# Sixteen tiles of attention's input, turned by VectorE's 32x32 blocks and transfers through DRAM instead of by TensorE

## The chip, the cores and the metric

One core of a Trainium2 chip. The metric is the device time of one execution in microseconds (us); lower is better. The kernel before takes 1691.37 us (median of three runs, 1691.37 to 1691.6).

## The reference

2048 tokens (4 sequences of 512), width 512, all float32. Each layer is added to a residual `x`:

```
x = x + 0.5*ffnA(norm(x))            # gated, hidden 2048, Walsh-Hadamard folded into W2
x = x + attn(norm(x))                # attn normalises once more, with gamma and beta, and adds its own input
x = x + 0.5*ffnA(norm(x))
x = x + 0.5*ffnB(norm(x))            # ternary weights, hidden 1408
x = x + ssm(norm(x))                 # tanh(x B^T) C^T + D x
x = x + 0.5*ffnB(norm(x))
```

with, in attention,

```
residual = x                                     # here x is norm(x) of the main path
x_norm = (x - mu) / sqrt(var + EPS) * gamma + beta
q, k, v = x_norm @ qkv ; causal softmax per sequence ; out @ o_proj + residual
```

The change concerns `x_norm` alone: attention needs it with features on the partitions, that is, turned.

## The kernel before

`x` stays in SBUF as 16 tiles of 128 tokens. A matmul in float32 quality is three passes over a high and a low part (`three`, lines L601, L603, L605), so each operand is split: ScalarE (ACT) writes the high part, VectorE (DVE) the low part (the source less the high part).

**The feed-forward passes.** `PASSES` lists eight; numbers 0 to 3 are ffnA on half the tokens each. A pass of kind A has 16 slots, one for each 128 hidden units. In a slot TensorE computes seven products of six matmuls (a Strassen-like scheme) in the order p1, p5, p6, p2, then four tiles of the down product (six matmuls each, in a ring of three PSUM banks), then p7, p3, p4. In the last slot p7, p3, p4 come ahead of the down tiles, and eight more down tiles follow. The seven products share five banks, so other engines stand between them: ACT copies BY to BW (`seed_w`, L1555) between p7 and p4, so **p4 can't start until ACT has run `seed_w`**, and ACT works its list strictly in order. Within a slot its list is `seed_y`, `hid_high`, `keep_p5`, (first normalisation), `silu_c11`, ..., (second normalisation), `seed_w`, `silu_c12`, `hid_high`. The order on every engine is that of the code; there is no planner for it. A value named `..._ready` or `..._done` is a semaphore.

**Weights** come from copies in DRAM (`w13_kept`, `w2_kept`), all through the queue of SyncE (SP), which also works strictly in order. In its iteration for slot s it loads the w13 weights of slot s+1 (896 KB of high parts in two transfers, 896 KB of low parts in one), then w2 of slot s. During pass 1 the weights of ffnB are prepared and stored as well, up to slot 12.

**The two normalisations ahead of attention** go in eight pairs of tiles, h = 0 to 7 (chunk c of attention, one sequence, is pairs 2c and 2c+1). `first_norm(h)` on ACT writes the main path's norm into `xn`; DVE's `second_stats(h)` takes its mean and variance; GpSimd (POOL) makes scale and shift and adds the norm to `x` (`y_added`); `second_norm(h)` on ACT writes attention's norm, still without gamma and beta, beside it (`xn[2:4]` for h < 4, `xnb` after). Pairs 0 to 3 are normalised in slots 12 to 15 of pass 1 (`TWICE_IN`), pairs 4 to 7 inside attention.

**Turning.** TensorE turns each tile by four 128x128 transposes against `ident` into a PSUM bank (`turn`, L937; semaphore `tt_ready`). Pairs 0 to 2 are turned in slots 13, 14, 15 (`TURNED_EARLY`) between or before down tiles, pair 3 right before the first q product, pairs 4 to 7 between attention's products (`x_turn`). ACT then applies gamma and beta in PSUM (`affine`, L1453) and writes `xt_hi` (L1460); DVE writes `xt_lo` (L2269).

**The other way of turning** is there already: after passes 0, 2 and 3, and in `s_turn` for the pass after attention, DVE transposes 32x32 blocks inside a tile (`STREAM_TRANSPOSE`), SP stores the result in DRAM and loads it back in another order of the blocks. Two tiles go together, since their elements are interleaved in pairs.

Of the kernel before, what the change touches and what calls it, by code (L numbers as in the profile page):

```python
# [8 lines left out]
F32 = mybir.dt.float32  # L9
# [6 lines left out]
P = 128  # L16
# [88 lines left out]
class Plan:  # L105
# [26 lines left out]
    def add_pass(self, no):  # L132
# [12 lines left out]
        for s in range(ps.n + 1):  # L145
# [13 lines left out]
            if no == BEFORE_T - 1:  # L159
                if s in TURNED_EARLY:  # L160
                    for j, b in enumerate((BV, BX)):
                        n = 2 * TURNED_EARLY.index(s) + j
                        self.bank["t", n] = b
                        ps.turns[s].append((n, n))
            elif no < len(PASSES) - 1 and no not in SWAPPED and s in ps.turn_slots:
# [64 lines left out]
def build(nc, t):  # L230
# [7 lines left out]
    s_scratch = nc.dram_tensor("s_scratch", [2, KD, 2 * P // BLOCK, BLOCK, P // BLOCK, 2 * BLOCK], F32).ap()  # L238
    mix_raw = nc.dram_tensor("mix_raw", [2, P, KD * D], F32).ap()
    mix_kept = nc.dram_tensor("mix_kept", [2, P, 2, KD * D], F32).ap()  # L240

    with ExitStack() as ctx:
# [52 lines left out]
        xnb = at("xnb", [P, 4, D], F32, "hid", 8 * KIB)  # L295
        s_swap = at("s_swap", [P, 2, KD, P // BLOCK, BLOCK, 2], F32, "hid", 8 * KIB)
# [58 lines left out]
        def bank(b):  # L355
# [58 lines left out]
        tt_ready, affine_ready, xt_hi_ready, xt_ready = (sem("tt_ready"), sem("affine_ready"), sem("xt_hi_ready"),  # L414
                                                         sem("xt_ready"))
# [12 lines left out]
        t_use = {("x", 1, 1): 0, ("q", 0, 0): 1, ("q", 0, 1): 2}  # L428
        for c in range(CH):
            extra = {0: [("x", 2, 0), ("q", 1, 0), ("x", 2, 1), ("q", 1, 1)],  # L430
                     1: [("x", 3, 0), ("q", 2, 0), ("x", 3, 1), ("q", 2, 1)],
                     2: [("q", 3, 0), ("q", 3, 1)], 3: []}[c]
            for key in [("v", c, 0), ("v", c, 1)] + extra:
                t_use[key] = len(t_use)
        products = [key for key in t_use if key[0] in "qv"]
        filled = {key: n + 1 for n, key in enumerate(products)}
# [156 lines left out]

        def first_norm_tile(h, j):
            return xn[:, j, :] if h < 4 else xn[:, 2 * (h % 2) + j, :]
# [19 lines left out]
        def _(sp):  # L615
# [151 lines left out]

            def s_turn(c):
# [67 lines left out]
            for ps in passes[1:]:  # L836
                if ps.no == BEFORE_T:
                    sp.wait_ge(mix_split_kept, 16 * len(MIX_IN))
                    sp.wait_ge(p4_done, T_UNITS)
                    for m in range(2):  # L840
                        sp.dma_start(mix_hi[m][:, :, :].rearrange("p k d -> p (k d)").bitcast(F32),
                                     mix_kept[m][:, 0, :]).then_inc(mix_in[m], 16)
                        sp.dma_start(mix_lo[m][:, :, :].rearrange("p k d -> p (k d)").bitcast(F32),
                                     mix_kept[m][:, 1, :]).then_inc(mix_in[m], 16)
                    for c in range(2):
                        s_turn(c)
                for s in range(ps.n):
# [45 lines left out]
        def _(pe):  # L893
# [79 lines left out]
            def first_product(ps, s, exact):  # L973
                u = ps.u0 + s
                weights_wait(ps, s, exact)
                if ps.no == BEFORE_T - 1 and s - 1 in TURNED_EARLY:
                    pe.wait_ge(xt_ready, 2 * TURNED_EARLY.index(s - 1) + 2)
# [99 lines left out]
            def turn_tiles(ps, s):  # L1077
                for n, tile in ps.turns[s]:
                    if ps.no == BEFORE_T - 1:
                        pe.wait_ge(p5_kept if plan.bank["t", n] == BV else c11_read, ps.u0 + s + 1)  # L1080
                        pe.wait_ge(xnb_ready, n + 1)
                        turn(t_tile(n), plan.bank["t", n]).then_inc(tt_ready, 1)
                    else:
                        bank_free("n", n)
                        pe.wait_ge(xn_ready, plan.norm_base[ps.no] + tile + 1)
# [1688 lines left out]
```

## Time and profile before

| | |
|---|---|
| median of three runs | 1691.37 us |
| the profiled execution | 1691.88 us |
| its span, first to last instruction | 1690.1 us |
| TensorE (PE) busy | 1681.5 us, 99% |
| VectorE busy | 1169.0 us, 69% |
| ScalarE busy | 821.5 us, 49% |
| DMA | 361.33 MB, mean 214 GB/s |

The profile is of one execution; its time outside the span is 1.8 us. A matmul's own duration (about 390 ns) overlaps its neighbours'; what a matmul costs is the distance from one start to the next, about 0.227 us for 128x512. Idle time of an engine other than TensorE costs nothing unless TensorE waits for it.

### The profile page before, as it was taken

Reading aid. Unit: us, or ns where it says so; the run is one execution under the profiler, and the core shown is the slowest. Engines: PE = TensorE matmul, PEld = TensorE weight load, DVE = VectorE, ACT = ScalarE, POOL = GpSimd, SP = SyncE. Lnnn points to the kernel's source line nnn. Section 1 sums busy time; section 2 is a strip of 40 time slices with the busy share of each in tenths; the row PEclk is TensorE's granted clock in tenths of the full one; section 3 lists DMA queues with packets and bytes.
Section 4 is the critical chain, followed back from the end, with each engine's and each line's share of the span. In section 5 each row is a group of like instructions: output and inputs, shape, how many; then the busy total and the mean of one; then the engine's idle time right before and its main releaser. Section 6 shows DMA issues by size and latency. Waiting matters only on the chain.

```text
span 1690.1 us, 21592 instructions
## 1 busy us (share of the span) xinstructions
PE 1681.5 (99%) x7579; PEld 1389.0 (82%) x7579; DVE 1169.0 (69%) x1832; ACT 821.5 (49%) x1335; POOL 125.6 (7%) x185
## 2 busy tenths in 40 slices
PE   9999999999999999999999999999999999999998
PEld 7788888888888888888888888888888888888887
DVE  8888778667776555755446655447668869877866
ACT  5745444465575543433223333223556456655644
POOL 1000000000012220000000000000000143100001
PEclk9999999999999999999999999999999999999999
DMA  9778866699985004257545457444766663366666
GB/s 319 265 309 298 288 261 230 242 366 361 369 336 212 1 1 99 96 175 224 180 154 184 153 173 239 144 160 147 254 226 206 252 224 112 131 233 240 250 222 214
DMA packets 140028, 361.33 MB, mean 214 GB/s; under 512 B 44688, under 2 KB 68112, under 8 KB 134544
## 3 DMA queue, kind: packets, MB, share of 16 engines
q1 hardware_dynamic: 139920, 359.92, 59.9%
q8 instruction: 64, 1.05, 0.3%
q14 instruction: 44, 0.36, 0.1%
HBM read 270.22 MB, written 89.65 MB: 213 GB/s over the span
## 4 chain that ended last, share of the span: by engine, by line
PE 94%; DVE 3%; DMA 1%; SPq 1%; issue 1%; ACT 0%; DVEq 0%; ACTq 0%
PE psum L601 35%; PE psum L603 30%; PE psum L605 27%; PE psum L937 1%; DMA x<-in_w2a 1%; SPq L748 1%; DVE xc_lo L2144 0%; DMA w<-w_kept 0%; DMA flat<-in_w3a 0%; PE psum L1214 0%; DVE att_lo L2113 0%; DVE fw_lo L2107 0%; SPq L704 0%; DVE x L2090 0%; DVE x L2202 0%
## 5 line engine op out<-in xcount | busy, mean ns | idle before, releaser
L601 PE MATMUL psum<-xc_hi,w 128*128 128x512 f32 x1544 | 603.8, 391 | 1.1 <-DMA w<-w_kept 0.6
L603 PE MATMUL psum<-xc_lo,w 128*128 128x512 f32 x1544 | 600.9, 389 | 0.0
L605 PE MATMUL psum<-xc_hi,w 128*128 128x512 f32 x928 | 361.2, 389 | 0.0
L601 PEld LDWEIGHTS psum<-xc_hi,w 128*128 128x128 f32 x1544 | 289.8, 188 | 66.1 <-issue 2.7
L603 PEld LDWEIGHTS psum<-xc_lo,w 128*128 128x128 f32 x1544 | 289.9, 188 | 59.2
L601 PE MATMUL psum<-w,hid 128*128 128x512 f32 x864 | 337.5, 391 | 0.0
L605 PE MATMUL psum<-w,hid 128*128 128x512 f32 x864 | 336.4, 389 | 0.0
L2186 DVE TENSOR_TENSOR x<-psum,x 128x512 f32<-128x512 f32 x256 | 173.1, 688 | 147.4 <-PE psum L605 146.8
L603 PE MATMUL psum<-w,hid 128*128 128x512 f32 x544 | 211.7, 389 | 0.0
L605 PEld LDWEIGHTS psum<-xc_hi,w 128*128 128x128 f32 x928 | 174.2, 188 | 36.4
L2210 DVE TENSOR_TENSOR hid<-sg,hid 128x512 fp32r<-128x512 f32 x212 | 144.6, 692 | 82.2 <-ACT hid L1516 79.7
L1555 ACT ACTIVATE psum<-psum 128x512 f32<-128x512 f32 x108 | 62.9, 582 | 284.8 <-PE psum L605 219.2
L601 PEld LDWEIGHTS psum<-w,hid 128*128 128x128 f32 x864 | 162.2, 188 | 36.2 <-DVE x L2186 2.7
L605 PEld LDWEIGHTS psum<-w,hid 128*128 128x128 f32 x864 | 162.2, 188 | 33.9
L1516 ACT ACTIVATE hid<-sg 128x512 fp32r<-128x512 f32 x204 | 129.3, 646 | 105.0 <-DVE sg L2236 51.9
L2227 DVE TENSOR_TENSOR sg<-psum,sg 128x512 f32<-128x512 f32 x104 | 71.6, 688 | 71.6 <-ACT psum L1555 70.8
L603 PEld LDWEIGHTS psum<-w,hid 128*128 128x128 f32 x544 | 102.2, 188 | 20.5
L2223 DVE TENSOR_TENSOR psum<-psum,sg 128x512 f32<-128x512 f32 x104 | 72.2, 695 | 42.8 <-PE psum L605 35.9
L1488 ACT ACTIVATE psum<-psum 128x512 f32<-128x512 f32 x108 | 62.8, 581 | 78.7 <-PE psum L605 53.6
L1954 POOL TENSOR_SCALAR var_eps<-meanvar 128x4 f32<-128x4 f32 x24 | 7.0, 291 | 1227.6 <-DVE meanvar L2058 854.1
L1547 ACT ACTIVATE sg<-psum 128x512 f32<-128x512 f32 x64 | 38.0, 594 | 89.2 <-PE psum L605 89.2
L1363 ACT ACTIVATE xn<-x,shift,rstd 128x512 f32<-128x512 f32 x88 | 65.7, 806 | 13.4 <-POOL shift L1957 10.0
(178 smaller groups left out, 2002.6 us busy)
## 6 DMA issues: line engine op xcount, KB each, us to landing
w<-w_kept SPq DMA_DIRECT2D x93, 896.0 KB, 6.7
w<-w_kept SPq DMA_DIRECT2D x130, 512.0 KB, 7.3
w<-w_kept SPq DMA_DIRECT2D x57, 640.0 KB, 4.5
w_kept<-w SPq DMA_DIRECT2D x16, 1792.0 KB, 7.4
w<-w_kept SPq DMA_DIRECT2D x93, 256.0 KB, 4.5
w_kept<-prep SPq DMA_DIRECT2D x12, 1792.0 KB, 7.5
w_kept<-w SPq DMA_DIRECT2D x16, 512.0 KB, 7.6
turn_scratch<-swap SPq DMA_DIRECT2D x48, 128.0 KB, 2.5
```

What stands on the lines that cost most here:

```text
L601: pe.matmul(out, a_hi, b_hi, start=start, stop=False, skip_group_check=onto)
L603: last = pe.matmul(out, a_hi, b_lo, start=False, stop=stop and zero == "a", skip_group_check=onto)
L605: last = pe.matmul(out, a_lo, b_hi, start=False, stop=stop, skip_group_check=onto)
L1363: return copy(out, x[:, i, :], AF.Identity, bias=shift[:, i:i + 1], scale=rstd[:, i:i + 1])
L1488: copy(bank(BY), bank(BX), AF.Copy).then_inc(y_seeded, 1)
L1516: copy(by_tile(hid_of(u, c)[:, 0, :], no), in_pairs(own(u) if c else sg[:, 0, :], no), AF.Copy).then_inc(hid_hi_ready, 1)
L1547: copy(sg[:, 0, :], bank(BX), AF.Silu, scale=gate_scale(ps, s)).then_inc(c11_read, 1)
L1555: copy(bank(BW), bank(BY), AF.Copy).then_inc(w_seeded, 1)
L2186: tt(at_x, b, at_x, ALU.add).then_inc(added, 1)
L2210: tt(by_tile(h[:, 1, :], no), in_pairs(source, no), by_tile(h[:, 0, :], no), ALU.subtract).then_inc(hid_ready, 1)
L2223: tt(bank(BZ), bank(BY), own(u), ALU.add).then_inc(z_seeded, 1)
L2227: tt(own(u), bank(BY), own(u), ALU.add).then_inc(c22_ready, 1)
```

## The change

All 16 tiles are turned the other way. For a pair h, now: `second_norm(h)` on ACT; `xt_swap_pair(h)` on DVE (two `STREAM_TRANSPOSE` of 128x512); `xt_store(h)` on SP (one transfer of 512 KB to `x_scratch`, in runs of 1 KB); `xt_load(h)` on SP (four transfers of 128 KB into `xt_raw`, in runs of 256 bytes); `xt_high(h)` on ACT (gamma and beta in place in SBUF by four instructions of 128x256, then one copy of 128x1024 to `xt_hi`); `xt_low(h)` on DVE (one subtraction of 128x1024). The 64 transposes on TensorE, their banks and their waits go.

```diff
+            def xt_store(h):
+                sp.wait_ge(xt_swapped, 2 * h + 2)
+                if h >= 2:
+                    sp.wait_ge(xt_in[raw_half(h - 2)], raw_loads(h - 2))
+                sp.dma_start(x_scratch[h % 2]..., xt_swap[...]...).then_inc(xt_stored[h % 2], 16)
+            def xt_load(h):
+                if h:
+                    sp.wait_ge(xt_ready, 2 * (h if h <= 4 else h - 1))
+                else:
+                    sp.wait_ge(kept2[(LAST_W2 - 1) % 4], nth(LAST_W2 - 1, 4))
+                sp.wait_ge(*stored(h))
+                for b in range(P // BLOCK):
+                    sp.dma_start(xt_raw[...]..., x_scratch[...]...).then_inc(xt_in[raw_half(h)], 16)
...
@@ SyncE, attention (mix loads: the weights of q and of v)
                     for m in range(2):
+                        if m:
+                            xt_load(3)
                         sp.dma_start(mix_hi[m]...) ; sp.dma_start(mix_lo[m]...)
+                    for h in (4, 6): store h, store h+1, load h, load h+1
@@ SyncE, pass 1
                             if s == UNITS["B"] + 1:          # slot 12
+                                xt_store(0)
                                 w2_out(LAST_W2)
+                                xt_load(0)
+                        elif s in TWICE_IN:                  # slots 13, 14, 15
+                            xt_store(TWICE_IN.index(s))
+                            if s + 1 < ps.n:
+                                xt_load(TWICE_IN.index(s))
@@ ScalarE
+            def xt_high(h):
+                act.wait_ge(xt_in[raw_half(h)], raw_loads(h))
+                for k in range(KD):
+                    last = copy(raw[:, k, :], raw[:, k, :], AF.Identity, bias=beta[...], scale=gamma[...])
...
+                copy(xt_cols(xt_hi, h), raw_cols(h), AF.Copy).then_inc(xt_hi_ready, 1)
             def first_norm(h):
...
+                if h == 5:
+                    act.wait_ge(xt_swapped, 2 * 4)
+                elif h:
+                    act.wait_ge(*stored(h - 1 if h < 5 else h - 2))
@@ ScalarE, up_slot
-                if ps.no == BEFORE_T - 1 and s in TWICE_IN:
-                    first_norm(TWICE_IN.index(s))
                 silu_c11(ps, s)
+                if ps.no == BEFORE_T - 1 and s in TWICE_IN[1:]:
+                    first_norm(TWICE_IN.index(s))
...
-                    if not last:
-                        turned_early(ps, s)
+                    if s in TURNED_EARLY and not last:
+                        xt_high(TURNED_EARLY.index(s))
                     if s in TWICE_IN and not last:
                         second_norm(TWICE_IN.index(s))
@@ VectorE, up_slot
+                if early and last:
+                    second_stats(TWICE_IN.index(s))          # ahead of sum_c22, gated
...
+                    if early and last and k < 2:
+                        xt_swap_pair(TWICE_IN.index(s), (k,)) # between the down tiles' adds
...
                     hid_low(u, 1)
+                    if early and s in TWICE_IN:
+                        xt_swap_pair(TWICE_IN.index(s))
                     hid_low(u, 0)
```

Three places of the order. ScalarE in slot 13 of pass 1, before, from the silu of the first gate (`silu_c11`) to `seed_w` (`psum<-psum`, waiting for p7_done); `psum,small` is gamma and beta, `kept...` are stores of weights:

```order
L1547 ACTIVATE sg<-psum 128x512 [waits hid_ready,p2_done]
L1453 ACTIVATE psum<-psum,small 128x128 [waits tt_ready]
L1453 ACTIVATE psum<-psum,small 128x128 x3
L1460 ACTIVATE xt_hi_78<-psum 128x4x128 [waits kept2_3,kept2_0,kept13_1,affine_ready]
L1453 ACTIVATE psum<-psum,small 128x128 [waits tt_ready]
L1453 ACTIVATE psum<-psum,small 128x128 x3
L1460 ACTIVATE xt_hi_78<-psum 128x4x128 [waits affine_ready]
L1479 ACTIVATE xn<-xn,shift_121,rstd_120 128x512 [waits tt_ready,rstd2_ready]
L1479 ACTIVATE xn<-xn,shift_121,rstd_120 128x512
L1555 ACTIVATE psum<-psum 128x512 [waits c21_read,p7_done]
```

and the same stretch of the changed kernel, in its own line numbers (L1390 is `first_norm`, L1479 and L1487 `xt_high`, L1507 `second_norm`, L1583 `seed_w`):

```order
L1575 ACTIVATE sg<-psum 128x512 [waits hid_ready,p2_done]
L1390 ACTIVATE xn<-x,shift,rstd 128x512 [waits xt_stored0,rstd_ready,stats2_ready,y_added]
L1390 ACTIVATE xn<-x,shift,rstd 128x512 [waits rstd_ready]
L1479 ACTIVATE xt_raw_85<-xt_raw_85,small 128x256 [waits xt_in0]
L1479 ACTIVATE xt_raw_85<-xt_raw_85,small 128x256 x3
L1487 ACTIVATE xt_hi_78<-xt_raw_85 128x4x256 [waits kept2_3,kept13_1,affine_ready]
L1507 ACTIVATE xn<-xn,shift_125,rstd_124 128x512 [waits xt_swapped,rstd2_ready]
L1507 ACTIVATE xn<-xn,shift_125,rstd_124 128x512
L1583 ACTIVATE psum<-psum 128x512 [waits c21_read,p7_done]
```

`first_norm` has moved behind the silu and waits for the store of the pair before; between it and `seed_w` ACT now waits for a load (`xt_in0`) where it waited for a turn of TensorE.

SyncE at slots 12 to 14 of pass 1, before (`prep` and `prep_last` are stores of ffnB's weights; `w_53` is w13, `w_54` w2):

```order
L698 DMA w_kept<-prep_68 128x1024 [waits w2_ready]
L698 DMA w_kept<-prep_last 128x1024 [waits w2_ready]
L617 DMA w_53<-w_kept 128x1280 [waits p4_done,kept13_0]
L617 DMA w_53<-w_kept 128x512
L649 DMA w_53<-w_kept 128x1792 [waits w13_lo_in0]
L663 DMA w_54<-w_kept 128x1024 [waits kept2_1,down_ready]
L617 DMA w_53<-w_kept 128x1280 [waits p4_done,kept13_1]
```

and now:

```order
L714 DMA w_kept<-prep_68 128x1024 [waits w2_ready]
L788 DMA x_scratch<-xt_swap_83 128x4x256 [waits xt_swapped]
L714 DMA w_kept<-prep_last 128x1024 [waits w2_ready]
L800 DMA xt_raw_85<-x_scratch 32x16x64 [waits xt_stored0,kept2_3]
L800 DMA xt_raw_85<-x_scratch 32x16x64 x3
L633 DMA w_53<-w_kept 128x1280 [waits p4_done,kept13_0]
L633 DMA w_53<-w_kept 128x512
L665 DMA w_53<-w_kept 128x1792 [waits w13_lo_in0]
L679 DMA w_54<-w_kept 128x1024 [waits kept2_1,down_ready]
L788 DMA x_scratch<-xt_swap_83 128x4x256 [waits xt_swapped]
L800 DMA xt_raw_85<-x_scratch 32x16x64 [waits xt_stored1,xt_ready]
L800 DMA xt_raw_85<-x_scratch 32x16x64 x3
```

The loads of the weights for slot 14 (the first L633) and slot 15 stand behind a wait for a store to land.

## Rows read from the trace of the kernel before

**Rows 1.** The page: busy time by engine, and the granted clock in 40 slices.

```profile
PE 1681.5 (99%) x7579; PEld 1389.0 (82%) x7579; DVE 1169.0 (69%) x1832; ACT 821.5 (49%) x1335; POOL 125.6 (7%) x185
...
PEclk9999999999999999999999999999999999999999
```

**Rows 2.** TensorE's timeline (start us, us, what, [idle before]): the warming matmuls.

```profile
1.33 5.06 PE L1298 MATMUL psum<-warm 128*128 128x512 f32 x11 [1.33 <-POOL warm L1931]
```

**Rows 3.** TensorE's timeline in slot 13: a turn between matmuls; start of p4.

```profile
496.83 0.39 PE L605 MATMUL psum<-w,hid 128*128 128x512 f32 x1
497.07 1.03 PE L937 MATMUL psum<-ident,xn 128*128 128x128 f32 x8
497.86 0.48 PE L601 MATMUL psum<-w,hid 128*128 128x512 f32 x1
498.17 0.40 PE L603 MATMUL psum<-w,hid 128*128 128x512 f32 x1
...
504.75 0.39 PE L601 MATMUL psum<-xc_hi,w 128*128 128x512 f32 x1
```

**Rows 4.** Groups of TensorE by form: the turns of `xnb`, busy us, mean ns.

```profile
L937 PE MATMUL psum<-ident,xnb 128*128 128x128 f32 x32 | 4.2, 273 | 0.0
```

**Rows 5.** VectorE's timeline: `hid_low` in slots 12 and 13; block transposes in `s_turn`.

```profile
491.26 0.69 DVE L2210 TENSOR_TENSOR hid<-sg,hid 128x512 fp32r<-128x512 f32 x1
...
507.01 0.69 DVE L2210 TENSOR_TENSOR hid<-sg,hid 128x512 fp32r<-128x512 f32 x1
...
653.89 2.48 DVE L2612 STREAM_TRANSPOSE s_swap<-xn 128x512 f32<-128x512 f32 x4
```

**Rows 6.** SyncE's timeline: issues at slots 12 and 14, and a turn in pass 3.

```profile
489.15 0.32 SPq L698 DMA_DIRECT2D w_kept<-prep  x1
494.32 0.32 SPq L698 DMA_DIRECT2D w_kept<-prep_last  x1
...
507.20 0.42 SPq L649 DMA_DIRECT2D w<-w_kept  x1
...
1034.14 2.60 SPq L760 DMA_DIRECT2D turn_scratch<-swap  x4
1039.23 1.75 SPq L765 DMA_DIRECT2D xs<-turn_scratch  x4
```

**Rows 7.** DMA issues in four windows, the last from the page: KB each, us to landing.

```profile
w_kept<-prep SPq DMA_DIRECT2D x1, 512.0 KB, 7.6
w_kept<-prep_last SPq DMA_DIRECT2D x1, 512.0 KB, 3.6
...
w<-w_kept SPq DMA_DIRECT2D x1, 896.0 KB, 6.5
...
s_scratch<-s_swap SPq DMA_DIRECT2D x2, 512.0 KB, 3.1
...
s_scratch<-s_swap SPq DMA_DIRECT2D x4, 512.0 KB, 4.4
...
turn_scratch<-swap SPq DMA_DIRECT2D x48, 128.0 KB, 2.5
```

**Rows 8.** ScalarE's timeline: slots 13 and 15, and an `affine` of 128x256.

```profile
501.71 1.51 ACT L1479 ACTIVATE xn<-xn,shift,rstd 128x512 f32<-128x512 f32 x2
503.59 0.58 ACT L1555 ACTIVATE psum<-psum 128x512 f32<-128x512 f32 x1 [0.37 <-PE psum L605]
...
527.64 0.60 ACT L1547 ACTIVATE sg<-psum 128x512 f32<-128x512 f32 x1 [0.72 <-PE psum L605]
...
582.88 1.91 ACT L1453 ACTIVATE psum<-psum,small 128x256 f32<-128x256 f32 x4 [0.38 <-PE psum L937]
```

**Rows 9.** Line L1394, a copy of 128x1024: duration ns min/median/max, first and last start.

```profile
L1394 ACT ACTIVATE xc_hi<-xs x40: 1041/1050/1084, 56.5 to 1572.1; 128x1024 fp32r<-128x1024 f32 x40
```

**Rows 10.** VectorE's timeline in slot 15: `sum_c22`, and the first down tile's add.

```profile
529.61 0.69 DVE L2227 TENSOR_TENSOR sg<-psum,sg 128x512 f32<-128x512 f32 x1 [1.09 <-ACT psum L1555]
...
534.04 0.68 DVE L2186 TENSOR_TENSOR x<-psum,x 128x512 f32<-128x512 f32 x1
```

More of the change, by code:

```diff
@@ L158, in add_pass @@
                         self.w2_slot_free[self.w2 + b + 4] = self.d - 1
[L159 to L165, printed above, removed]
+            if BEFORE_T <= no < len(PASSES) - 1 and no not in SWAPPED and s in ps.turn_slots:
                 for j in range(2):
@@ L592, in p_at, with first_norm_half, stored, raw_half @@
             return i % 2 if c + 1 < CH else i
+        def first_norm_half(h):
+            return 0 if h < 4 else h % 2
         def first_norm_tile(h, j):
-            return xn[:, j, :] if h < 4 else xn[:, 2 * (h % 2) + j, :]
+            return xn[:, 2 * first_norm_half(h) + j, :]
+        def stored(h):
+            return xt_stored[h % 2], 16 * (h // 2 + 1)
+        def raw_half(h):
+            return h % 2 if h >= 4 else 0
+        def raw_loads(h):
+            return LANDED * sum(raw_half(i) == raw_half(h) for i in range(h + 1))
+        def xt_cols(tile, h):
+            return tile[h // 2 % 2][:, :, h % 2 * 2 * P:(h % 2 + 1) * 2 * P].rearrange("p k (i t) -> p k i t", i=2)
+        def raw_cols(h):
+            return xt_raw[raw_half(h)][:, :, :].rearrange("p k (t i) -> p k i t", i=2)
         block = ctx.enter_context(nc.Block())
@@ L1445, in low_parts @@
                          accum_out=low_sum[:, 3 * k + i:3 * k + i + 1]).then_inc(low_ready, 1)
-            affined = [0]
-            def affine(tiles):
+            def xt_high(h):
+                raw = xt_raw[raw_half(h)]
+                act.wait_ge(xt_in[raw_half(h)], raw_loads(h))
                 for k in range(KD):
-                    part = ps_[:, tiles, k * P:(k + 1) * P]
-                    last = copy(part, part, AF.Identity, bias=beta[:, k:k + 1], scale=gamma[:, k:k + 1])
+                    last = copy(raw[:, k, :], raw[:, k, :], AF.Identity, bias=beta[:, k:k + 1], scale=gamma[:, k:k + 1])
                 last.then_inc(affine_ready, 1)
-                affined[0] += 1
-                act.wait_ge(affine_ready, affined[0])
-            def xt_high(n, b):
-                c, i = n // TT, n % TT
-                copy(xt_hi[c % 2][:, :, i * P:(i + 1) * P], bank(b).rearrange("p (k t) -> p k t", k=KD),
-                     AF.Copy).then_inc(xt_hi_ready, 1)
+                act.wait_ge(affine_ready, h + 1)
+                if h == 0:
+                    act.wait_ge(kept13[W13_BASE["S"] % 2], nth(W13_BASE["S"], 2))
+                    act.wait_ge(kept2[(LAST_W2 - 1) % 4], nth(LAST_W2 - 1, 4))
+                if h == 2:
+                    act.wait_ge(kept2[LAST_W2 % 4], nth(LAST_W2, 4))
+                copy(xt_cols(xt_hi, h), raw_cols(h), AF.Copy).then_inc(xt_hi_ready, 1)
             def first_norm(h):
@@ L1584, in up_slot @@
                     w13_split(s + 1)
-                if ps.no == BEFORE_T - 1 and s in TWICE_IN:
-                    first_norm(TWICE_IN.index(s))
+                if ps.no == BEFORE_T - 1 and s == TWICE_IN[0]:
+                    first_norm(0)
                 if preparing and s == 1:
@@ L1619, in up_slot @@
                     mix_high(MIX_IN.index(s))
+                if last and ps.no == BEFORE_T - 1:
+                    second_norm(TWICE_IN.index(s))
                 if last:
@@ L1628, in up_slot @@
                     hid_high(u, 1)
-                if last and ps.no == BEFORE_T - 1:
-                    second_norm(TWICE_IN.index(s))
-            def turned_early(ps, s):
-                for n, _ in ps.turns[s]:
-                    b = plan.bank["t", n]
-                    act.wait_ge(tt_ready, n + 1)
-                    affine(b)
-                    if n == 0:
-                        act.wait_ge(kept13[W13_BASE["S"] % 2], nth(W13_BASE["S"], 2))
-                        act.wait_ge(kept2[(LAST_W2 - 1) % 4], nth(LAST_W2 - 1, 4))
-                        act.wait_ge(kept2[LAST_W2 % 4], nth(LAST_W2, 4))
-                    xt_high(n, b)
             def seed(ps, i):
@@ L2305, in up_slot @@
                         convert(following, 2 + k // 2)
-                    if early and ps.turns[s] and k >= 2:
-                        n, _ = ps.turns[s][k - 2]
-                        xt_low(n, plan.bank["t", n])
+                    if early and s in TWICE_IN[1:] and not last and k == 0:
+                        second_stats(TWICE_IN.index(s))
+                    if early and s in TURNED_EARLY and k == TT - 1:
+                        xt_low(TURNED_EARLY.index(s))
+                    if early and last and k < 2:
+                        xt_swap_pair(TWICE_IN.index(s), (k,))
                 if last:
```

127 lines of the change are left out of this document (56 added, 71 removed).

## Prediction

> **What bounds the kernel now.** I read the page first. TensorE is busy 1681.5 of 1690.1 us [rows 1], so all its waits together are 8.6 us: what it executes sets the time, and nothing but its own work can be saved. The granted clock is the full one, 2.4 GHz, in all 40 slices. TensorE's list of waits comes next: the longest is 1.33 us, at the start of the span [rows 2], and no wait stands at pass 1's end or in attention. So the reader is to see two things: each transpose that leaves TensorE shortens the time one for one, and any wait put in its place lengthens it one for one. Then TensorE's timeline for the price of a turn, the order for who now waits for whom, and the timelines of the other engines and of the DMA for when that wait ends.
>
> **What is removed.** From the start of the matmul ahead of a turned pair to the start of the second one behind it are 498.17 - 496.83 = 1.34 us [rows 3]; without the turn these are two distances of 0.227 (L603 to L605 in a stream), 0.45. So a pair costs 0.89 us. The other pairs in slots 14, 15 and before q show the same pattern, those in attention 0.87. Eight pairs: **7.0 us saved**. The group line gives 131 ns for each of the 32 turns of `xnb` [rows 4], 8.4 us for 64; the difference is overlap at the edges, and I keep 7.0.
>
> The mean duration in that line is 273 ns. The Trainium skill (TensorE: Matmul & The Clock Gate, Part 4) gives about 275 ns for such a transpose within a kernel, and agrees with the row as a duration. Taken as the cost it would make 64 x 0.275 = 17.6 us saved; but the trace has eight turns from 497.07 to 497.86, 0.10 each, so durations overlap and the sum doesn't go by it.
>
> **What is added, slot 13.** Before, ACT waited between silu and `seed_w` for TensorE's turn and had time left. Now it waits there for the load of pair 0, and p4 waits for `seed_w`. The chain:
> - VectorE's `hid_low` of slot 12 ends at 491.26 + 0.69 = 491.95; two block transposes at 2.48/4 = 0.62 [rows 5] end at 493.2. SyncE issues the store at 493.3.
> - The queue is full of stores of weights there: one issued at 489.15 lands 7.6 us later, at 496.75, and the next of 512 KB, issued at 494.32, lands 3.6 later, at 497.9 [rows 6, 7]. That is 1.2 us behind the other although issued 5.2 later: transfers come out in the order in which they went in. The new store takes that place, so it lands at 497.9. Bounds: 3.6 after issue (496.9) and 7.6 (500.9).
> - Four loads of 128 KB in 256-byte runs. The trace has no such load, but stores of that shape: from the first issue at 1034.14 to the wait's end at 1039.23 are 5.1 us; the four issues take 2.6, the last starts about 2.0 in, and lands 2.5 later by the median [rows 6, 7], 4.5. I take 4.8 (bounds 4.5 and 6.0): 502.7.
> - ACT then: gamma and beta, four instructions of 128x256, 1.9 as in PSUM (in SBUF only 128x512 is shown, 1.5 for two, and half the columns can't cost more: bounds 1.5 and 3.0); the copy of 128x1024 1.05 [rows 9]; `second_norm` 1.5; `seed_w` 0.58 [rows 8]; with overlap at the edges 4.9 in all: 507.6, p4 at 507.7.
> - Without the turn TensorE would come to p4 at 504.75 - 0.89 = 503.86 [rows 3]. **It waits 3.9 us** (from 2.5, with both lower bounds, to 8).
>
> **Slot 14.** Counted from the slot's first matmul, which stood at 504.75 + 1.36 = 506.1: `hid_low` ends at 507.70, +1.6 [rows 5]; transposes +2.85; store issued +2.95. The queue is quiet now, so it lands 3.1 later [rows 7], +6.05; loads +0.1 + 4.8, +10.95; ACT 4.9, +15.85. TensorE comes to p4 after 60 matmuls, +13.6. **2.2 us** (bounds 1.3 and 4.9, the upper with 4.4 for the store and 6.0 for the loads). The first normalisation, behind the silu, is done long before the load and costs nothing.
>
> **Slot 15.** Nothing is loaded ahead of `seed_w`, but `first_norm(3)` stands there. The slot starts at 522.0 in before; the silu at 527.64 [rows 8], +5.6, and leaves ACT at +6.1, as store 2 lands; the two norms take until +7.6, `seed_w` until +8.2 where p4 comes at +8.16: 0.1 us. More costs VectorE's new order: `second_stats(3)` stands ahead of `sum_c22`, needs these norms, and takes 1.6, so `sum_c22` starts at +9.2 instead of 529.61, +7.6 [rows 10]. POOL's four small steps (1.7) and `second_norm(3)` (1.5) end at +12.4, and only then comes ACT's `hid_high` (0.65), so `hid_low` ends at +13.8, and the first down tile's add at +14.5 instead of 534.72, +12.7. The down tiles have three banks: the fourth waits for the first's add, and would start at +13.7. 0.8 us. Two transposes and `xt_low` between the adds push a later add 0.2 past its tile. **1.1 us** (0.3 to 2.5).
>
> A matmul behind a wait costs 0.31 instead of 0.23 to the next [rows 3]; four such, **0.3 us**.
>
> **The weights behind the round trip.** SyncE now issues slot 14's weights after the loads, at 497.9 + 2.7 = 500.6 instead of 494.7. Their last part is issued 0.9 later and takes 6.5 [rows 6, 7]: 508.0, for a slot that would start at 505.2 but starts at 509.1 through ACT's wait. For slot 15: +8.7, landing +16.1, against a start at +15.0 + 2.2. Both are covered, by 1.1 us each, by a wait that is paid already. If that cover is gone, the weights are the bound: without any wait on ACT they still cost 2.8 and 1.1.
>
> **At nothing.** Attention: pair 3's load is issued behind half of the mix weights, about 19 us into slot 15's time, and lands at +27, with the q product ending at +32; the mix weights of q land at +25, with q starting at +27, those of v 6 us ahead. Pair 4 and 5: transposes end 4.1 us after v's second product starts, when VectorE had statistics to do which have moved behind; loads land at 10.7 and 13.2 after that start, the q product of the next chunk ends at 13.5 and is followed by 10 us of matmuls in banks already free. Slot 12: two transposes delay `hid_low`, needed two slots later. DMA: 8 x 1 MB more in 361 MB.
>
> **Sum.** -7.0 + 3.9 + 2.2 + 1.1 + 0.3 = +0.5. Against the profiled execution's 1691.88 that is 1692.4; it lies 0.5 over the median of 1691.37, for which the forecast is **1691.9 us: no change** that a measurement of this kernel can tell (0.2%, 3.4 us).
>
> **Rivals.**
> - *The round trips are hidden.* Speaks for it: in passes 0, 2 and 3 twelve such turns cost TensorE no wait. Against it: there nothing on ACT's list waits for them in the same slot. It needs `xt_in` 8.7 us after the slot's start, where I have 10.95, and slot 13's earlier still. With all waits gone 1684.4; with the weights as the bound (2.8 + 1.1, and slot 15's 1.1) 1689.7.
> - *Slower: each crossing of DRAM is slow.* Place: ACT at `xt_in` in slots 13 and 14, and at `xt_stored` in slot 15. With others in flight the same stores took 4.4 instead of 3.1 [rows 7], and the queue's order may be less kind than one row suggests. With 1.3 more on stores and 1.2 more on loads: 2.5 + 2.5 + 1.3 = 6.3 more, **1698.2**. It is slower than noise once the crossings together run 2.9 us over mine. Since ACT's list is in order, nothing absorbs it.
> - *The clock falls.* The waits in slot 13 would be three times the longest of before, which stood at the start of the span, and behind which the warming matmuls took 5.06 us for 11 [rows 2], 0.46 each instead of 0.227. If slot 13's wait brought the same back for as many matmuls, 11 x 0.23 = 2.5 us: 1694.4. [...]
> - *The change doesn't do what it says*: the order has no turn of these tiles on TensorE left, so only the first step could be off by its price.
>
> **Chances.** Forecast 0.50 (0.04 faster, 0.40 same, 0.06 slower); hidden 0.17 (0.13 faster, 0.04 same); slow crossings 0.22 (0.19 slower, 0.03 same); clock 0.11 (0.06 same, 0.05 slower). Together faster 0.17, same 0.53, slower 0.30. Range 1686.5 to 1698.5: it leaves out the fully hidden case (0.07) and the slower half of the slow one (0.11). The forecast's own is 1689 to 1695.
>
> **What would show it.** TensorE 64 matmuls fewer (7515). Its waits: p4 in slot 13 on `seed_w` near 3.9 us, in slot 14 near 2.2, a down tile in slot 15 near 0.8 on VectorE; ACT idle before `xt_raw` on a DMA in both slots. Wrong would be: waits on `w<-w_kept` at the first product of slots 14 or 15; any wait in attention; a clock under 1.00 after slot 13; no wait at p4.

## Result and profile after

| | before | changed |
|---|---|---|
| median, runs in turn on one chip (22 of each) | 1692.74 us | 1695.7 us |
| the profiled execution | 1691.88 us | 1694.74 us |
| its span | 1690.1 us | 1692.9 us |
| TensorE busy | 1681.5 us | 1676.4 us |

The ratio is 1.0016 (95% interval 1.001 to 1.0022): 0.16% slower, some 2.7 us. That is within the 0.2% that I had called no change, though the interval excludes none at all. The forecast was +0.5 us.

The page of the changed kernel, its busy line, answers [rows 1]: 64 matmuls fewer, as they should be.

```profile
PE 1676.4 (99%) x7515; PEld 1382.7 (82%) x7515; DVE 1176.8 (70%) x1840; ACT 820.0 (48%) x1315; POOL 127.3 (8%) x185
```

TensorE's list of waits in the changed kernel (line, what for: us in total, times, longest). L1583 is `seed_w`; L2198 the add of a down tile:

```profile
PE psum L617 <- ACT psum L1583: 6.2, 2, 4.5
PE psum L1325 <- POOL warm L1943: 1.3, 1, 1.3
PE psum L617 <- DVE x L2198: 1.2, 1, 1.2
PE psum L617 <- DMA w<-w_kept: 1.2, 2, 1.0
```

The first and the third are new, and they are where the prediction had put them. (The 1.0 us on weights stands near 1594 us, far behind the change.) TensorE's timeline shows the first of them, p4 of slot 13 (start us, us, what, [idle before]):

```profile
503.30 0.39 PE L619 MATMUL psum<-xc_lo,w 128*128 128x512 f32 x1
503.52 0.39 PE L621 MATMUL psum<-xc_hi,w 128*128 128x512 f32 x1
508.40 0.79 PE L617 MATMUL psum<-xc_hi,w 128*128 128x512 f32 x1 [4.49 <-ACT psum L1583]
509.00 0.63 PE L619 MATMUL psum<-xc_lo,w 128*128 128x512 f32 x1
509.42 0.63 PE L621 MATMUL psum<-xc_hi,w 128*128 128x512 f32 x1
...
511.13 0.55 PE L617 MATMUL psum<-xc_hi,w 128*128 128x512 f32 x1
511.51 0.40 PE L619 MATMUL psum<-xc_lo,w 128*128 128x512 f32 x1
511.75 0.40 PE L621 MATMUL psum<-xc_hi,w 128*128 128x512 f32 x1
...
524.71 0.39 PE L621 MATMUL psum<-xc_hi,w 128*128 128x512 f32 x1
526.76 0.50 PE L617 MATMUL psum<-xc_hi,w 128*128 128x512 f32 x1 [1.66 <-ACT psum L1583]
```

Read starts, not durations. From 503.52 to 508.40 are 4.88 us where 0.227 is usual: 4.65 lost. And what follows is a second loss that no list of waits names: the next matmuls start 0.60, then 0.42 to 0.43, then 0.38 us apart, and only from 511.51 on 0.23 again. These seven distances are 3.11 us where 1.59 is usual: 1.5 lost. The windows of the changed kernel (busy us of PE, PEld, DVE, ACT, POOL, granted clock, DMA share, GB/s) say what it is:

```profile
504.00:508.40 4.40, 0.00 (x0) 0.00 (x0) 1.24 (x2) 4.37 (x8) 1.31 (x2) 0.96 1.01 401
508.40:509.50 1.10, 1.10 (x3) 0.91 (x4) 1.00 (x2) 0.47 (x1) 0.00 (x0) 0.50 0.46 186
509.50:511.70 2.20, 2.20 (x7) 1.75 (x6) 0.64 (x2) 0.67 (x1) 0.00 (x0) 0.56 0.05 19
511.70:520.00 8.30, 8.30 (x38) 6.81 (x38) 5.30 (x9) 3.77 (x6) 0.00 (x0) 1.00 0.40 111
```

TensorE had done nothing from 503.9 to 508.4; the granted clock falls within that stretch and is half, 1.2 GHz, when p4 begins. TensorE is "busy" all the while that it runs at half the clock, so busy time hides the loss.

Slot 14's p4 starts 2.05 us after the matmul ahead of it (1.8 lost), without a fall of the clock. In slot 15 the fourth down tile starts 1.63 us after the matmul ahead of it, which is at 541.80 (1.4 lost):

```profile
543.43 0.50 PE L617 MATMUL psum<-w,hid 128*128 128x512 f32 x1 [1.24 <-DVE x L2198]
```

**The account.** A measure free of what happens elsewhere is the stretch from slot 13's first down matmul to attention's first q matmul: 495.70 to 549.53 before, 53.8 us, and 495.59 to 555.80 in the changed kernel, 60.2. Four turned pairs fell out of it, at 0.88 each 3.5, so without any wait it would be 50.3. The 9.9 above are 4.65 + 1.5 + 1.8 + 1.4, and 0.5 in single matmuls that start 0.33 to 0.34 after one that had waited, and in smaller differences. Attention, from its first q matmul to the first matmul of the pass behind it, took 153.4 and now takes 149.7: 3.6 back for its four pairs, 0.9 each, and nothing is lost there. 6.4 - 3.6 = 2.8; the span is 2.9 longer.

ScalarE's timeline of the changed kernel, slot 13:

```profile
498.00 1.52 ACT L1390 ACTIVATE xn<-x,shift,rstd 128x512 f32<-128x512 f32 x2 [1.61 <-DMA x_scratch<-xt_swap]
503.24 2.08 ACT L1479 ACTIVATE xt_raw<-xt_raw,small 128x256 f32<-128x256 f32 x4 [3.71 <-DMA xt_raw<-x_scratch]
505.35 1.12 ACT L1487 ACTIVATE xt_hi<-xt_raw 128x1024 fp32r<-128x1024 f32 x1
506.37 1.50 ACT L1507 ACTIVATE xn<-xn,shift,rstd 128x512 f32<-128x512 f32 x2
507.77 0.58 ACT L1583 ACTIVATE psum<-psum 128x512 f32<-128x512 f32 x1
```

and SyncE's, of the same kernel, against [rows 6]:

```profile
493.55 0.37 SPq L788 DMA_DIRECT2D x_scratch<-xt_swap  x1
494.72 0.32 SPq L714 DMA_DIRECT2D w_kept<-prep_last  x1
497.92 3.10 SPq L800 DMA_DIRECT2D xt_raw<-x_scratch  x4
501.12 0.90 SPq L633 DMA_DIRECT2D w<-w_kept  x2
502.06 0.43 SPq L665 DMA_DIRECT2D w<-w_kept  x1
```

The store was issued at 493.55 (predicted 493.3), had landed at 497.92 (497.9), and ACT got the load at 503.24 (502.7). Slot 14's weights were issued at 501.12 instead of 494.74.

### The profile page after: what moved, and what is told of

It is laid out like the page before. It is cut to its first block, busy times and chain, and to the rows that moved or that the text cites. A ratio compares the mean times of both kernels' runs of the same rounds, so it can differ in the third digit from the quotient of the medians.

```text
span 1692.9 us, 21495 instructions
## 1 busy us (share of the span) xinstructions
PE 1676.4 (99%) x7515; PEld 1382.7 (82%) x7515; DVE 1176.8 (70%) x1840; ACT 820.0 (48%) x1315; POOL 127.3 (8%) x185
## 4 chain that ended last, share of the span: by engine, by line
PE 91%; DVE 3%; DMA 2%; SPq 1%; issue 1%; ACT 1%; POOL 0%; ACTq 0%; DVEq 0%; POOLq 0%
PE psum L617 34%; PE psum L619 29%; PE psum L621 26%; PE psum L987 1%; DMA x<-in_w2a 1%; SPq L764 1%; DVE xc_lo L2156 0%; DMA x_scratch<-xt_swap 0%; DMA w<-w_kept 0%; DMA xt_raw<-x_scratch 0%; DMA flat<-in_w3a 0%; DVE att_lo L2125 0%; PE psum L1253 0%; DVE fw_lo L2119 0%; ACT xn L1507 0%
## 5 line engine op out<-in xcount | busy, mean ns | idle before, releaser
L2198 DVE TENSOR_TENSOR x<-psum,x 128x512 f32<-128x512 f32 x256 | 172.6, 687 | 145.5 <-PE psum L621 145.0
L1583 ACT ACTIVATE psum<-psum 128x512 f32<-128x512 f32 x108 | 62.9, 582 | 283.4 <-PE psum L621 217.1
L1544 ACT ACTIVATE hid<-sg 128x512 fp32r<-128x512 f32 x204 | 129.6, 647 | 103.2 <-DVE sg L2248 52.5
L1516 ACT ACTIVATE psum<-psum 128x512 f32<-128x512 f32 x108 | 62.8, 581 | 80.1 <-PE psum L621 54.6
L1390 ACT ACTIVATE xn<-x,shift,rstd 128x512 f32<-128x512 f32 x88 | 65.8, 808 | 12.7 <-POOL shift L1969 7.2
```

Of the source, the lines that this page charges most:

```text
L1390: return copy(out, x[:, i, :], AF.Identity, bias=shift[:, i:i + 1], scale=rstd[:, i:i + 1])
L1516: copy(bank(BY), bank(BX), AF.Copy).then_inc(y_seeded, 1)
L1544: copy(by_tile(hid_of(u, c)[:, 0, :], no), in_pairs(own(u) if c else sg[:, 0, :], no), AF.Copy).then_inc(hid_hi_ready, 1)
L1583: copy(bank(BW), bank(BY), AF.Copy).then_inc(w_seeded, 1)
L2198: tt(at_x, b, at_x, ALU.add).then_inc(added, 1)
```

## Experiments

All stretches are from slot 13's first down matmul to attention's first q matmul: 53.8 before, 60.2 changed, 50.3 without a wait (the forecasts below were made with 50.6). Each run is of the changed kernel with the edit shown; ratios are to the kernel before on the same chip.

**clock_kept.** Does the stillness alone bring the clock down?

```diff
@@ TensorE, between p3 and p4, slot 13
+                    pe.wait_ge(c11_read, u + 1)
+                    ...
+                    for n in range(IDLE_MATMULS):            # 18
+                        pe.matmul(bank(BX), w13[...], xc_hi[...], start=True, stop=True)
                 pe.wait_ge(w_seeded, u + 1)
```

> The changed kernel with 18 more matmuls of 128x512 on TensorE in slot 13 alone, between the third and the fourth product, into the bank that the next slot's first product starts anew; nothing reads them. In the changed kernel TensorE stood still there for 4.88 us (503.52 to 508.40) and its next eight matmuls came 0.60, 0.42 to 0.43 and 0.38 us apart instead of 0.23, 1.7 us in all, at a granted clock of 0.50 to 0.56. Theory (the stillness alone brings the clock down, the wait itself is ACT's): the 18 matmuls take 4.1 us of the 4.88 and leave less than 1 us idle, the fourth product begins at the same time as before them and its matmuls come 0.23 us apart, the granted clock of 508.4 to 511.7 is 1.00, and the whole is 1.5 to 1.8 us shorter than the changed kernel (0.09 to 0.11%). Rival (the clock falls for another reason, such as the load of transfers at 400 GB/s in the same stretch): the eight matmuls stay at 0.42 and nothing is gained. Second rival (more matmuls disturb the conversions' timing): the fourth product starts later than 508.6.

Stretch 62.0, ratio 1.0016 (1.0007 to 1.0025). TensorE's timeline of clock_kept, slots 13 and 14:

```profile
502.41 4.24 PE L1084 MATMUL psum<-xc_hi,w 128*128 128x512 f32 x18
506.89 0.50 PE L618 MATMUL psum<-xc_hi,w 128*128 128x512 f32 x1 [0.24 <-ACT psum L1590]
507.23 0.39 PE L620 MATMUL psum<-xc_lo,w 128*128 128x512 f32 x1
...
521.78 0.39 PE L622 MATMUL psum<-xc_hi,w 128*128 128x512 f32 x1
524.50 0.80 PE L618 MATMUL psum<-xc_hi,w 128*128 128x512 f32 x1 [2.34 <-ACT psum L1590]
525.09 0.63 PE L620 MATMUL psum<-xc_lo,w 128*128 128x512 f32 x1
525.52 0.63 PE L622 MATMUL psum<-xc_hi,w 128*128 128x512 f32 x1
```

The cause was right, the gain wrong. In slot 13 the clock stayed at 1.00 (507.23 follows 506.89 by 0.34, all others by 0.23), under the same load of transfers (393 GB/s from 502 to 507, as in the changed kernel from 503.5 to 508.4). But p4 still starts when ACT lets it. Counted from the start of the stretch, TensorE comes to slot 14's p4 1.6 us sooner than in the changed kernel, but that p4 starts only 0.9 sooner, since the round trip is not sooner by as much: 2.72 us between two matmuls, and the clock fell there. Slot 15's p4 waits as well, for 1.0 us; in the changed kernel it did not.

**clock_kept_two.** The same with 9 more such matmuls in slot 14.

> The changed kernel with matmuls nobody reads in both early waits: 18 ahead of the fourth product of slot 13 and 9 ahead of that of slot 14. Measure: the stretch from slot 13's first down matmul to attention's first q matmul, 53.8 us before the change, 60.2 in the changed kernel, 62.0 with the 18 alone, where the second wait grew to 2.7 us and the low clock (eight matmuls at 0.43) came behind that one instead. Theory (the chain store, load, ACT sets the time of each fourth product, and the low clock is a cost on top wherever a wait is over some 2.5 us): no matmul at 0.43 us is left, slot 14's fourth product starts when it did with the 18 alone, and the stretch is 62.0 less 1.7 to 1.9, that is 60.1: no better than the changed kernel, since what the clock gives back in slot 13 the chain takes in slots 14 and 15. Rival (the clock's 1.7 us are simply a term of the sum): the stretch is 58.5.

Stretch 60.2 (forecast 60.1), ratio 1.0013 (1.0004 to 1.0023); no matmul at 0.43 us is left. So the low clock is a real cost (1.5 us in the changed kernel, 1.7 in clock_kept), but removing it gives only the right to wait longer. Against the changed kernel slot 13's p4 starts 0.5 later in the stretch, slot 14's loses 0.3 more and slot 15's 0.75: together the 1.5 that the clock gave back.

**seed_first.** Is the order on ACT the cause?

```diff
@@ ScalarE, slots 13 and 14
+                if seed_before:                              # slots 13, 14
+                    seed_w(u)
                     xt_high(...) ; ... ; second_norm(...) ; ...
-                seed_w(u)
+                if not seed_before:
+                    seed_w(u)
```

> The changed kernel with one order changed on ACT in slots 13 and 14: seed_w ahead of xt_high and second_norm. Theory (TensorE's fourth product waited because seed_w was queued behind xt_high, which waits for the transfer): the waits of 4.49 and 1.66 us on seed_w are gone, and with them the 1.7 us at low clock behind the first. But ACT is still held by the transfer until about 506.4 and then has second_norm, silu_c12, a hid conversion and the next slot's seed_y in its queue, so the next product that needs ACT, the third of slot 14 (p6, due at 507.8), is late next: by 0 to 3.3 us. Sum: 4.65 + 1.7 + 1.8 less 3.3 + 1, that is 1 to 8 us shorter than the changed kernel, likeliest 4 (1690.7 us profiled against 1694.7). Rival (the order is not the cause: TensorE would have stood for the transfer's share of DMA or for weights): the wait moves to w_kept's weights and the gain is under 1 us.

A miss: stretch 60.9, ratio 1.0022 (1.0013 to 1.0031). Waits of TensorE in seed_first (L1516 is `seed_y`):

```profile
PE psum L617 <- DMA w<-w_kept: 4.5, 4, 3.5
PE psum L617 <- ACT psum L1516: 2.3, 1, 2.3
...
PE psum L617 <- ACT psum L1583: 0.8, 1, 0.8
```

and its timeline at slot 14's first product, the matmul ahead of it being at 505.44:

```profile
509.36 0.47 PE L617 MATMUL psum<-xc_hi,w 128*128 128x512 f32 x1 [3.54 <-DMA w<-w_kept]
```

p4 of slot 13 waits for ACT no more, and 1.3 us later slot 14's first product waits 3.5 us for its weights (a distance of 3.92, with the clock down behind it). The rival was right: the last part of the weights, issued behind the round trip, lands at 509.1. Two chains of nearly one length ended in slot 13; the list of waits shows only the one that came last. The 2.3 us on the next `seed_y` are in slot 15.

**no_round_trip.** Is it the serial way through DRAM, or the bytes?

```diff
@@ SyncE, xt_load
-                sp.wait_ge(*stored(h))
                 for b in range(P // BLOCK):
-                    sp.dma_start(xt_raw[...], x_scratch[h % 2]...)
+                    sp.dma_start(xt_raw[...], t["x"][b * BLOCK:(b + 1) * BLOCK, :, h * 2 * BLOCK:(h + 1) * 2 * BLOCK])
```

> Leaves out the round trip's dependence: the four loads of each pair read 256-byte runs of the input x in DRAM, as many bytes in as many runs, instead of what the store wrote, and do not wait for the store; so what attention works on is not its input. The stores stay. Theory (the lost time of slots 13 and 14 is the serial chain store, load, ACT): the first load starts 4.4 us earlier, lands near 498 to 500 instead of 503.2, ACT's seed_w comes before 504.5, TensorE waits under 0.8 us in slot 13 and not at all in slot 14, no low clock; 7.5 to 8.2 us shorter than the changed kernel, that is 1686.5 to 1687.2 us profiled and a ratio of 0.996 to 0.997 to the kernel before; the DVE wait of 1.2 us in slot 15 may stay. Rival (it is the bytes on the queues, not the order): loads and weights still collide at 400 GB/s, the wait stays over 3 us.

A miss for slot 13, right for slot 14: stretch 58.8, ratio 1.0004 (0.9996 to 1.0013). ScalarE and SyncE in no_round_trip:

```profile
495.43 3.03 SPq L799 DMA_DIRECT2D xt_raw<-in_x  x4
```

```profile
501.68 2.08 ACT L1478 ACTIVATE xt_raw<-xt_raw,small 128x256 f32<-128x256 f32 x4 [3.32 <-DMA xt_raw<-in_x]
...
518.73 2.08 ACT L1478 ACTIVATE xt_raw<-xt_raw,small 128x256 f32<-128x256 f32 x4 [0.33 <-DMA xt_raw<-in_x]
```

The stretch begins 1.0 us earlier here (494.56). Counted from it, the load is issued 1.5 us sooner than in the changed kernel and lands 0.5 sooner (7.1 against 7.65): it takes 6.25 us instead of 5.3. It runs beside its pair's store (landed at 496.7), which is the likely reason, not one shown by itself. The edit took away one wait of two: `xt_load(0)` also waits for an earlier store of weights, which landed at 495.41, so the load could not go 4.4 us sooner, as expected. p4 still starts 4.35 us after its forerunner, and the clock falls, for twelve matmuls. In slot 14, with empty queues, the wait is gone. So in slot 13 the rival is nearer: with the full queues the wait for the pair's own store is worth only 0.5 us there. How long the load would take in slot 13 with nothing beside it, no run shows.

**one_slot_later.** Give the round trip a whole slot.

```diff
@@ ScalarE and VectorE: slots 14, 15 take pairs 0, 1; attention takes pairs 2, 3
-                        xt_high(TURNED_EARLY.index(s))
+                        xt_high(TURNED_EARLY.index(s) - 1)
@@ SyncE: loads 1, 2 behind the next slot's weights; load 3 behind the mix weights
```

> The changed kernel with the affine and conversion of each early pair (xt_high, xt_low) one slot later, 14 and 15, pair 2 in attention, and each load behind the next slot's weights in SP's queue. Theory: a pair's round trip then has a whole slot (16 us) and ends about 10 us before ACT asks, so no wait on seed_w in slots 13 and 14 (6.15 us), no low clock (1.7 us) and what stays is slot 15's 1.2 us on DVE; 8 us shorter than the changed kernel: 1686.7 us profiled, ratio 0.9965 (0.9955 to 0.998) to the kernel before. Rival (the weights behind the round trip or attention's start then bind): pair 2, which attention now converts at its start, delays the first q product, or the later loads push the mix weights, and 1 to 4 us of it come back (ratio 0.998 to 1.0).

A miss: stretch 62.4, ratio 1.0042 (1.0029 to 1.0055). Waits of TensorE:

```profile
PE psum L617 <- DMA w<-w_kept: 4.8, 5, 3.4
PE psum L617 <- DMA mix_lo<-mix_kept: 3.4, 1, 3.4
```

ACT's share fell from 6.2 us to 1.0. What came in its place is SyncE's order: load 0 was still ahead of slot 14's weights (issued at 502.51), and the mix weights, at 549.4, were behind load 2, which had to wait for slot 15's conversion. The clock fell behind both waits (distances of 3.75 and 3.82), for another 1.4 and 1.3 us.

**later_behind_weights.** Both moved: the conversions as in one_slot_later, and now load 0 too behind slot 14's weights.

```diff
@@ SyncE
                                 w2_out(LAST_W2)
-                                xt_load(0)
...
@@ SyncE, attention: the mix weights, then xt_load(2), xt_load(3)
```

> The changed kernel with each early pair converted one slot later, as in the run one_slot_later, and now the first load too behind slot 14's weights in SP's queue, and attention's mix weights ahead of the loads of pairs 2 and 3. In one_slot_later the 3.4 us on w_kept in slot 14, 1.7 us at low clock behind them, 3.4 us on mix_lo and 1.7 us at low clock behind those came from the first load still standing ahead of slot 14's weights (issued at 502.5, at 494.7 before the change) and from the mix weights behind load 2. Theory: those four go; left are 1.0 us on seed_w in slot 13 (second_norm, which waits for POOL and through it for the store), 0.2 in slot 15 and 1.4 on DVE: the stretch is 50.6 + 1.2 + 0.2 + 1.4 = 53.4 us, against 60.2 in the changed kernel, and the whole 1687 to 1688.5 us profiled, ratio 0.9965 to 0.998. Rival (the 256-byte transfers slow the weights wherever they stand): 1 to 3 us on w_kept stay, the stretch is 55 to 57.

The stretch came out at 53.9 (forecast 53.4), with 1.05 and 0.3 on `seed_w`, 1.24 on the add, and nothing on weights. The whole did not: ratio 1.0041 (1.0026 to 1.0056). All is lost behind the stretch, 9.8 us on `q_lo` in two waits of up to 8.2, and the clock fell in the second, to half for 10.2 us. I had put the conversions of pairs 2 and 3 ahead of q's on ACT and VectorE. Load 2 landed only at 554.8, behind 4 MB of mix weights issued from 537.9 on, and load 3, which waits for pair 2's conversion to free the buffer, was issued at 559.4 and landed at 565.0.

**slot_15_order.**

```diff
@@ ScalarE, slot 15
-                    second_norm(3)
                     hid_high(u, 0)
                     convert(following, 3)
+                    second_norm(3)
@@ VectorE: the two block turns one down tile later
```

> The changed kernel with slot 15's second_norm on ACT behind the hid conversion instead of ahead of it, and the two block turns on DVE one down tile later. Theory: in the changed kernel ACT waited 2.5 us for POOL in second_norm with the hid conversion behind it (541.20), DVE waited 2.4 us for that conversion (541.88) and the first down add came at 542.70, so the fourth down tile waited 1.24 us for its bank. With the order changed the conversion comes at about 539.5, the first add at 541, no wait on x, and the stretch is 60.2 less 1.4, 58.8 us; 1.2 to 1.4 us in all. Rival (the statistics ahead of the sums on DVE, not ACT's order, are what is late): the first add comes after 542.3 and over 0.8 us of the wait stay.

Stretch 58.8, as forecast; no wait on the add is left; ratio 1.0005 (0.9996 to 1.0015), against 1.0016 for the change. The statistics ahead of `sum_c22`, which this edit leaves where they were, were not it. Two things moved in this run, but the block turns stand behind the first down tile's add, for which the fourth tile waited. In the changed kernel that add is the last link here (`hid_high` is L1544, the add L2198):

```profile
539.77 1.53 ACT L1507 ACTIVATE xn<-xn,shift,rstd 128x512 f32<-128x512 f32 x2 [2.54 <-POOL shift L1982]
541.20 0.65 ACT L1544 ACTIVATE hid<-sg 128x512 fp32r<-128x512 f32 x1
...
541.88 0.90 DVE L2222 TENSOR_TENSOR hid<-sg,hid 128x512 fp32r<-128x512 f32 x1 [2.39 <-ACT hid L1544]
542.70 0.68 DVE L2198 TENSOR_TENSOR x<-psum,x 128x512 f32<-128x512 f32 x1
```

With the order changed `hid_high` starts at 538.39 and the add at 540.32, in a stretch that begins 1.0 us earlier.

**all_mended.**

```diff
@@ the two edits before, and
+        xt_swap_low = at("xt_swap_low", ..., "sp", 4 * KIB)      # pairs 0 to 2
@@ ScalarE, first_norm
+                elif 0 < h < 4:
+                    act.wait_ge(xt_swapped, 2 * h)
```

> later_behind_weights and slot_15_order together, and for pairs 0 to 2 a buffer of its own for the turned tiles, so that first_norm of the next pair waits for the block turns alone and no longer for the store to land. Theory: first_norm of slots 13 to 15 comes up to 2 us earlier, second_norm does not hold seed_w, and all the added waits are gone: stretch 50.6 to 51.2 us (60.2 in the changed kernel, 53.8 before), profiled time 1684.5 to 1686.5, ratio 0.9955 to 0.997. Rival (what the transposes took on TensorE covered something else, weights above all, which are now late by it): 1 to 3 us come back on w_kept in slots 14 and 15, ratio 0.997 to 0.9985.

Stretch 52.6, the wait on `seed_w` gone, 1.6 us on `w_kept` at slot 14's start: the rival, by its lower end. The whole still has the attention fault, 9.6 us on `q_lo`, ratio 1.0038 (1.0024 to 1.0052):

```profile
560.79 0.47 PE L621 MATMUL psum<-mix_hi,xt_hi 128*128 128x512 f32 x1 [2.85 <-DVE q_lo L2602]
...
573.30 0.48 PE L621 MATMUL psum<-xt_hi,q_hi 128*128 128x128 f32 x1 [6.78 <-DVE q_lo L2602]
```

The first of these is 3.24 us behind its forerunner, and the granted clock of 560.8 to 566.1 is 1.00: no fall. The second is 7.17 behind; there the clock fell within the wait, at 569.8.

**mended_attention and mended_store_later.**

```diff
@@ SyncE: mix weights, then xt_store(3), xt_load(2), xt_load(3)
@@ ScalarE (VectorE likewise), attention
-                xt_high(3)
                 pair_hi(("q", 0, 0), q_hi)
+                xt_high(2)
...
                 pair_hi(("q", 0, 1), q_hi)
+                xt_high(3)
@@ mended_store_later also, SyncE: w13_load(s + 1), w2_load(s), then xt_store(h), xt_load(h)
```

> all_mended, with attention's start in another order: SP issues the mix weights ahead of the store of pair 3 and the loads of pairs 2 and 3 behind both, and ACT and VectorE convert pair 2 behind the first q pair and pair 3 behind the second, instead of ahead of them. In all_mended the stretch (slot 13's first down matmul to attention's first q matmul) was 52.6 us against 60.2 in the changed kernel and 53.8 before, but in attention TensorE then stood 2.9 and 6.8 us for q_lo, whose conversion was queued behind pair 2 (landed 554.9) and pair 3 (563.7). Theory (only that queue order costs): both waits are gone, the stretch is 52.6 or less, and attention keeps its 3.5 us of transposes less: 1.2 + 3.5 = 4.7 us under the kernel before, 1685.4 us profiled span, ratio 0.9972 (0.9965 to 0.998), faster than both kernels. Rival (pairs 2 and 3 now come too late for the second chunk's q products near 615, or the mix weights move the loads so far): 1 to 5 us come back after 600.

> mended_attention with the stores of pairs 0 to 2 behind the next slot's weights as well in SP's queue. In all_mended TensorE still waited 2.4 us on w_kept in slots 14 and 15 (1.6 the longest), with slot 14's weights issued at 493.93 behind the 512 KB store of pair 0. Theory (those 512 KB ahead of the weights are 1.2 us of transfer time at 410 GB/s): the waits on w_kept fall from 2.4 to under 1.2 us, and the whole is another 1.2 us shorter, ratio 0.9965. Rival (TensorE is now at the rate at which weights arrive, whatever stands ahead of them): the waits stay within 0.4 us of 2.4.

Ratios 0.9969 (0.9956 to 0.9981) and 0.9966 (0.9954 to 0.9978): **both faster than the kernel before**, 1687.1 and 1686.6 us against 1691.9 on that chip, and by their ratios faster than the changed one (1.0016). Stretches 52.75 and 51.1. Waits of TensorE in mended_store_later, and SyncE's first issues there:

```profile
PE psum L621 <- DMA w<-w_kept: 1.8, 5, 0.5
PE psum L1328 <- POOL warm L1948: 1.3, 1, 1.3
```

```profile
495.24 0.32 SPq L718 DMA_DIRECT2D w_kept<-prep_last  x1
495.66 1.20 SPq L637 DMA_DIRECT2D w<-w_kept  x2
...
498.06 0.71 SPq L792 DMA_DIRECT2D x_scratch<-xt_swap_low  x1
508.24 1.91 SPq L804 DMA_DIRECT2D xt_raw<-x_scratch  x4
```

Slot 14's weights are issued at once again, and store and load stand behind them. The load's result is used in slot 14, at 513.46, one us after it landed, and nobody waits for it. The 1.7 us on the weights at slot 14's start in mended_attention became 0.2; what moved is the 512 KB store that had stood ahead of them. As whole kernels the two can't be told apart. Of the 7 us that the transposes were worth, 5.3 are in hand by the medians. In the profiled execution, the slowest of six, some 2 us come back after attention has begun, partly within it (it takes 150.6 us, against 149.7 in the changed kernel; distances of 0.39 to 0.49 stand around 564 and 572) and partly in short waits on weights in later passes. Their causes stay open.

## Why the prediction was right, and where it was not

- **What bounds the kernel; what is removed** [rows 1, 3]. Right: 0.88 us for each of the four early pairs, 3.6 us for the four in attention, 7.1 against 7.0. The 275 ns that the Trainium skill (TensorE: Matmul & The Clock Gate, Part 4) gives are for bfloat16, and these transposes are float32, so that they lie near the 273 of [rows 4] shows little. The price rests on the starts, and these bore it out.
- **Slot 13.** The mechanism was right: p4 on `seed_w`, through the load. It was mis-sized by a fifth: 4.65 against 3.9. Of the 0.75, the load was 0.5 longer than the 4.8 taken from [rows 6, 7] (5.3, within its bounds), and ACT took 5.1 from the load to the end of `seed_w`, where I had 4.9. VectorE, SyncE and the store were right to 0.3. The store landed where "transfers come out in the order in which they went in" had put it, but that is no rule: in mended_attention the first load, issued at 497.89, landed at 505.91, and a load of weights issued ahead of it, at 497.36, landed at 508.46.
- **The clock.** This is the largest part of the way from +0.5 to +2.8: 1.5 us, beside 0.75 more in slot 13, 0.4 less in slot 14 and 0.3 more in slot 15. It was a rival with a chance of 0.11 and 2.5 us, worked out from the eleven slow matmuls of [rows 2]; seven slow distances came. The fault is in how it was weighed. The forecast had the wait of 3.9 us in it, three times the longest in the trace, so the fall belonged to the forecast and not beside it. Distances of 4.88, 4.62 (slot_15_order), 4.35, 3.92, 3.82 and 3.75 us between two matmuls brought the clock to half, and so did one of 2.72 (clock_kept, slot 14), while 3.24 (all_mended), 2.65 (seed_first, slot 15) and 2.05 did not. So the "over some 2.5 us" with which clock_kept_two was forecast is not borne out either.
- **Slot 14.** 1.8 against 2.2, by the same chain. Its upper bound was added up wrongly (2.2 + 1.3 + 1.2 is 4.7, not 4.9), which changes nothing.
- **Slot 15.** 1.4 against 1.1, at the tile and by the engine named. Of the chain given for it, `hid_high` behind `second_norm(3)` was the part that mattered: slot_15_order took the wait away entirely and left `second_stats` where it was.
- **The weights behind the round trip.** "Covered by 1.1 us each by a wait that is paid already" was borne out by seed_first: with the cover gone in slot 13, 3.5 us at once, where 2.8 had been given.
- **Attention at nothing.** Right in the changed kernel, and fragile: another order at its start cost 9.8 and 9.6 us in waits, in two runs.
- **The hidden case**, 0.17, did not come in the changed kernel. The last kernel, in another order, gets 5.3 of the 7.0 us.

The forecast, no change within 0.2%, held at 0.16%, with 0.04% to spare, and the sum behind it was 2.3 us short. The mechanisms were right; that the missing 1.5 us of the clock did not carry the time over the line is luck.

## What to carry to other kernels

Replacing work on the bound engine by a round trip through DRAM pays only if its consumer stands far enough down every in-order list it touches: here one slot later on ACT and VectorE, and behind the next slot's weights on SyncE. Where a wait is removed, look for a second chain that ends within a microsecond or two of it (here the weights), and move both. And a forecast that puts a wait of several us on TensorE must put the low clock behind it into the sum, while padding the wait with idle matmuls buys little when the chain that ends it goes on to set the next wait.

## What was not expected of the hardware

- The clock fell with a distance of 2.72 us between two matmuls in one run and did not with 2.65 and 3.24 in others. Where matmuls of 128x512 followed, they came mostly 0.43 us apart, seven to twelve of them, for a loss of 1.3 to 1.7 us, once 2.5. It need not be down when TensorE resumes: in one_slot_later matmuls started again at 510.73, and the clock was 1.00 until 511.8 and 0.50 after. What the chip looks at is not settled by these runs.
- Four loads of 128 KB in 256-byte runs took 5.3 us from first issue to use with a store landing ahead of them, and 6.25 when begun 1.5 us sooner beside it. The four issues took 1.9 us on SyncE with the store already landed (mended_store_later, 508.24) and 3.1 at slot 12's end.
- ACT's `Identity` with scale and bias on 128x256 in SBUF took 2.08 us for four, against 1.91 in PSUM [rows 8]: no gain from leaving PSUM.
